# A fused linear-attention layer on one core: three reorderings and a last projection split in columns

## What is computed

```python
xn = layernorm(x)                                   # over the width
q, k, v = (silu(xn @ W) for W in (Wq, Wk, Wv))      # 16 heads of 16
# chunked linear attention with a decay per head, S carried over the chunks:
#   o = ((q k^T) * D) v  +  (q S) * q_decay ;  S = chunk_decay * S + (k * k_decay)^T v
o = o * sigmoid((xn @ Wg1) @ Wg2)                   # the gate
o = o * rsqrt(mean(o*o over the 16 of a head) + eps) * norm_w
s = o @ Wo
g = silu(fp8(xn * scale) @ fp8(W2 * scale1) / (scale * scale1))
out = x + s * g
```

## Time and profile before

| | |
|---|---|
| median of 3 runs | 128.74 us (128.6 to 129.91) |
| the profiled execution | 128.68 us, its span 126.9 us, so 1.78 us lie around the span |
| busy in the span | PE 114.7 us (90%), DVE 101.7 (80%), ACT 81.4 (64%), POOL 80.8 (64%) |
| granted TensorE clock | 0.99 of full speed over the span; the last fortieth of the span shows 7 tenths |
| DMA | 7.57 MB, mean 60 GB/s |
| steps 1 to 6 | VectorE makes og at 28.05, 41.56, 54.99, 68.40, 81.97, 95.32 and 108.68 us: 13.3 to 13.6 us a step |

### The profile page before, as it was taken

The page is one execution under the profiler, slowest core; times in us unless marked ns, Lnnn a source line. Parts: engine busy times, 40 slices in busy tenths (PEclk is TensorE's granted clock), DMA queues, the critical chain, the costliest instruction groups (busy, mean ns, idle before and its releaser), DMA issues.

```text
span 126.9 us, 6394 instructions
## 1 busy us (share of the span) xinstructions
PE 114.7 (90%) x2688; PEld 99.3 (78%) x2688; DVE 101.7 (80%) x271; ACT 81.4 (64%) x156; POOL 80.8 (64%) x119
## 2 busy tenths in 40 slices
PE   3979989988999999999999999999999999867680
PEld 3979889758978898879978898889788987556560
DVE  1899999989895899869994999498939891497781
ACT  7689989969967656684677378558673664811100
POOL 6716599899839683968677884968384839100070
PEclk9999999999999999999999999999999999999997
DMA  2769800020000400033003300150006040000015
GB/s 84 235 175 339 273 3 3 5 45 6 5 0 10 83 0 5 5 62 108 3 5 65 111 0 5 41 132 5 0 20 150 5 126 5 5 5 5 0 67 181
DMA packets 11067, 7.57 MB, mean 60 GB/s; under 512 B 4832, under 2 KB 11040, under 8 KB 11040
## 3 DMA queue, kind: packets, MB, share of 16 engines
q1 hardware_dynamic: 11040, 7.17, 20.2%
HBM read 3.50 MB, written 2.10 MB: 44 GB/s over the span
## 4 chain that ended last, share of the span: by engine, by line
POOL 31%; issue 29%; DVE 20%; ACT 9%; PE 6%; DMA 2%; POOLq 0%; DVEq 0%
POOL e_q L408 5%; POOL e_sum L403 5%; POOL y L441 5%; POOL kd L419 4%; DVE probs L764 4%; POOL rstd L396 3%; POOL own_mid L423 2%; POOL qd L413 2%; DMA x_sb<-in_L_attn_x_dram 2%; POOL on_lo L446 1%; PE b_s L1307 1%; DVE bn L729 1%; POOL own_end L423 1%; DVE og L797 1%; DVE xqT L754 1%
## 5 line engine op out<-in xcount | busy, mean ns | idle before, releaser
L1092 PE MATMUL b_kv<-w_hi,xT_hi 128*128 128x256 f32 x64 | 16.8, 284 | 0.0
L1093 PE MATMUL b_kv<-w_lo,xT_hi 128*128 128x256 f32 x64 | 16.5, 281 | 0.0
L441 POOL TENSOR_TENSOR y<-sg,x_sb 128x512 f32<-128x512 f32 x7 | 9.0, 1286 | 10.4 <-DVE sg L902 10.3
L446 POOL TENSOR_TENSOR on_lo<-on,on_hi 128x512 fp32r<-128x512 f32 x6 | 7.7, 1278 | 12.3 <-ACT on_hi L620 12.3
L403 POOL TENSOR_TENSOR e_sum<-e_y,e_magic 128x512 f32<-128x512 f32 x8 | 10.3, 1285 | 7.2 <-DVE e_magic L748 7.2
L797 DVE SCALAR_TENSOR_TENSOR og<-gate_tanh,b_o 128x512 f32<-128x512 f32 x7 | 4.8, 687 | 11.8 <-PE b_o L1243 11.8
L1095 PE MATMUL b_kv<-w_hi,xT_lo 128*128 128x256 f32 x64 | 12.7, 280 | 0.0
L1243 PE MATMUL b_o<-probs,v_par 64*32 64x64 f32 x896 | 12.6, 222 | 0.0
L413 POOL TENSOR_TENSOR qd<-q_silu,q_decay 128x512 f32<-128x512 f32 x8 | 10.3, 1293 | 3.3 <-ACT q_silu L550 3.3
L1092 PEld LDWEIGHTS b_kv<-w_hi,xT_hi 128*128 128x128 f32 x64 | 12.0, 188 | 0.2 <-issue 0.2
L1093 PEld LDWEIGHTS b_kv<-w_lo,xT_hi 128*128 128x128 f32 x64 | 12.1, 188 | 0.0
(11 more groups left out here) (205 smaller groups left out, 366.6 us busy)
## 6 DMA issues: line engine op xcount, KB each, us to landing
out_dram<-y SPq DMA_DIRECT2D x7, 256.0 KB, 2.5
x_sb<-in_L_attn_x_dram SPq DMA_DIRECT2D x4, 384.0 KB, 5.4
own_cross<-own_end SPq DMA_DIRECT2D x12, 64.0 KB, 2.0
qd_cross<-qd SPq DMA_DIRECT2D x12, 64.0 KB, 2.4
x_sb<-in_L_attn_x_dram SPq DMA_DIRECT2D x2, 256.0 KB, 3.5
w_f<-in_L_attn_Wq_dram SPq DMA_DIRECT2D x1, 256.0 KB, 3.8
w_f<-in_L_attn_Wk_dram SPq DMA_DIRECT2D x1, 256.0 KB, 4.0
w_f<-in_L_attn_Wv_dram SPq DMA_DIRECT2D x1, 256.0 KB, 4.5
```

The costliest lines, as they stand in the source:

```text
L441: g.tensor_tensor(y[:, n % 2], sg[:, n % 2].rearrange("p (s d) -> p s d", s=S), x_sb[:, x_tiles(n), :], ALU.add).then_inc(s_y, 1)
L446: g.tensor_tensor(on_lo[:], on[:, n % 2], on_hi[:].bitcast(F32), ALU.subtract).then_inc(s_onlo, 1)
L1092: t.matmul(dst[:, s], xT_hi[:, u, kk, tok], w_hi[:, w, kk], start=(s == 0 and kk == 0), stop=False, skip_group_check=True)
L1093: t.matmul(dst[:, s], xT_hi[:, u, kk, tok], w_lo[:, w, kk], start=False, stop=False, skip_group_check=True)
```

## The change

It has five parts. (1) In the steps 1 to 6 TensorE does the first quarter of the product with V (`from_chunk(n, 0, 0)`) ahead of `gate(n + 1)`, so that the gate's product stands next to `transpose_x(n + 2)`; step 6 has no transposes of x. (2) At the start ScalarE does `silu_v(0)` ahead of `silu_q(0)`, and `find_over(1)` ahead of `gate(1)`. (3) Still at the start, `gate_o(0)` goes ahead of `low_xT(2)` on VectorE, and `square_o(0)` ahead of `scale_y(2)` on ScalarE. (4) In step 7 VectorE does `gate_o(7)` ahead of `root_pair_last(6)`. (5) The last projection is done in three pieces (`LAST`): tile 0 whole, tile 1 in two halves of 128 columns, each with its own product, addition and store.

```diff
+        LAST = [(0, slice(0, D), b_s[:, 0:D], b_kv[:, 0:D]),
+                (1, slice(0, D // 2), b_s[:, 512:512 + D // 2], b_kv[:, 512:512 + D // 2]),
+                (1, slice(D // 2, D), b_o[:, 512:512 + D // 2], b_kv[:, 512 + D // 2:512 + D])]
...
-            for s in range(S):
-                sp.wait_ge(s_lasty, s + 1)
-                sp.dma_start(out_v[:, last.start + NB * s, :], y[:, 2, s]).then_inc(s_laststored, 16)
+            for m in range(len(LAST)):
+                s, cols, ps, prod = LAST[m]
+                sp.wait_ge(s_lasty, m + 1)
+                sp.dma_start(out_v[:, last.start + NB * s, cols], y[:, 2, s, cols]).then_inc(s_laststored, 16)
...
-            silu_q(0)
             act.wait_ge(s_vzero, 2)
             silu_v(0)
+            silu_q(0)
             high_xT(1)
...
+            find_over(1)
             gate(1)
-            find_over(1)
             high_xT(2)
             act.wait_ge(s_dvec, 4)
             silu_ffn(1)
+            square_o(0)
             scale_y(2)
-            square_o(0)
             silu_ffn(0)
...
             stats(3)
+            gate_o(0)
             low_xT(2)
-            gate_o(0)
...
             root_last(n - 1)
+            gate_o(n)
             root_pair_last(n - 1)
-            gate_o(n)
             head_norm(n - 1)
...
-            for s in range(S):
-                product_last(s)
-                add_x_last(s)
+            for m in range(len(LAST)):
+                product_last(m)
+                add_x_last(m)
...
+            def project_o_last(m):
+                n = STEPS - 1
+                s, cols, ps, prod = LAST[m]
+                pe.wait_ge(s_onlast, s + 1)
+                for kk in range(KH):
+                    mm = t.matmul(ps, on[:, n % 2, kk, s * P:s * P + P], wo_scaled[:, kk, cols], start=(kk == 0),
                                   stop=(kk == KH - 1), skip_group_check=True)
                 mm.then_inc(s_outps, 1)
...
                 state_steps(n)
+                from_chunk(n, 0, 0)
                 gate(n + 1)
-                from_chunk(n, 0, 0)
                 if known(n + 2):
                     transpose_x(n + 2)
```

More of the change, by code:

```diff
@@ L884, in head_norm_last, with product_last, add_x_last @@
                                 ps_rs.rearrange("p k (s c t) -> p s k c t", s=S, c=2)[:, s], ALU.mult).then_inc(s_onlast, 1)
-            def product_last(s):
+            def product_last(m):
                 n = STEPS - 1
-                dve.wait_ge(s_outps, n * S + s + 1)
+                s, cols, ps, prod = LAST[m]
+                dve.wait_ge(s_outps, n * S + m + 1)
                 dve.wait_ge(s_ffn, n + 1)
-                cols = slice(s * D, s * D + D)
-                v.tensor_tensor(ps_prod_last[s], ps_last[s], ffn_silu[:, n % 3, cols], ALU.mult).then_inc(s_lastsg, 1)
-            def add_x_last(s):
+                v.tensor_tensor(prod, ps, ffn_silu[:, n % 3, s * D + cols.start:s * D + cols.stop], ALU.mult).then_inc(s_lastsg, 1)
+            def add_x_last(m):
                 n = STEPS - 1
-                dve.wait_ge(s_lastsg, s + 1)
-                v.tensor_tensor(y[:, 2, s], ps_prod_last[s], x_sb[:, x_tiles(n).start + NB * s, :], ALU.add).then_inc(s_lasty, 1)
+                s, cols, ps, prod = LAST[m]
+                dve.wait_ge(s_lastsg, m + 1)
+                v.tensor_tensor(y[:, 2, s, cols], prod, x_sb[:, x_tiles(n).start + NB * s, cols], ALU.add).then_inc(s_lasty, 1)
             def product(n):
@@ L1279, in project_o @@
             def project_o(n, s):
-                if n == STEPS - 1:
-                    pe.wait_ge(s_onlast, s + 1)
-                elif s == 0:
+                if s == 0:
                     pe.wait_ge(s_on, n + 1)
@@ L1290, in project_o @@
                         pe.wait_ge(s_probs, 4 * STEPS)
-                dst = ps_out[:, s] if n < STEPS - 2 else ps_out_last2[:, s] if n < STEPS - 1 else ps_last[s]
+                dst = ps_out[:, s] if n < STEPS - 2 else ps_out_last2[:, s]
                 if n < STEPS - 2:
@@ L1306, in project_o @@
                 for kk in range(KH):
-                    mm = t.matmul(dst, on[:, n % 2, kk, s * P:s * P + P], wo_scaled[:, kk], start=(kk == 0 and (s == 0 or n == STEPS - 1)),
+                    mm = t.matmul(dst, on[:, n % 2, kk, s * P:s * P + P], wo_scaled[:, kk], start=(kk == 0 and s == 0),
+                                  stop=(kk == KH - 1), skip_group_check=True)
+                mm.then_inc(s_outps, 1)
+            def project_o_last(m):
+                n = STEPS - 1
+                s, cols, ps, prod = LAST[m]
+                pe.wait_ge(s_onlast, s + 1)
+                for kk in range(KH):
+                    mm = t.matmul(ps, on[:, n % 2, kk, s * P:s * P + P], wo_scaled[:, kk, cols], start=(kk == 0),
                                   stop=(kk == KH - 1), skip_group_check=True)
@@ L1413, in _ @@
             keep_warm(3, b_k)
-            for s in range(S):
-                project_o(n, s)
+            for m in range(len(LAST)):
+                project_o_last(m)
 _INS = ['L0_attn_x', 'L0_attn_log_decay', 'L0_attn_Wq', 'L0_attn_Wk', 'L0_attn_Wv', 'L0_attn_Wo', 'L0_attn_Wg1',
```

4 lines of the change are left out of this document (1 added, 3 removed).

## The result

| | before | after |
|---|---|---|
| median | 129.17 us (4 runs, 128.6 to 129.91) | 131.59 us (4 runs, 130.57 to 132.2) |
| ratio | | 1.0197, 95% interval 1.0128 to 1.0266 |
| the profiled execution | 128.68 us, span 126.9 | 132.2 us, span 130.5 |

The change costs 2.4 us. The forecast was 129.5 (+0.8), its range ended at 130.4: the sign was right, the size was not. The two profiled executions lie 3.5 apart, more than the medians: that of before is among the fastest of its kernel, that of after is the slowest of four. (A ratio leaves out executions more than 1.5% above the fastest of their kernel; where the clock falls in some executions of a kernel, that cuts some of these, so the medians over all stand beside the ratios.)

The account below looks back on a forecast made before the run. The prediction took a ring of og, VectorE and TensorE branches, then TensorE alone, to bound full steps. From 128.68 us, -0.4 (full steps) + 0.2 (start) + 0.9 (step 7) + 0.1 (tail) gave 129.5; range 128.5 to 130.4.

Parts of the forecast that it names:

- the 1.07: Step 7, TensorE: work in us from the load of spread_rs(6) to that of the head sums, without idle time.
- Rival C: Step 7: TensorE's clock falls after 1.8 us idle, work behind doubles, +2.2 us, 131.7 us; chance 0.05.
- The arrival of 0.3 of xT_hi's lateness: Start: xT_hi comes 0.4 us later, of which 0.3 reaches the projections of step 1.
- takes back: Start: find_over(1) ahead of the tanh recovers up to 0.48 us; xqT taken as 0.2 earlier than 25.98.
- the ring: Full steps: og, VectorE to last probs beside TensorE to state_steps, then TensorE alone to next og; at most 0.75 us saved.
- the only thing late next: Full steps: on_lo's slack of 0.12 us in step 2 limits the gain to 0.065 each in four steps.
- Rival A: Only full steps and start count as meant: 0.75 and 0.3 us saved, end costs 1.0, 128.6 us; chance 0.18.
- covered: Tail: part of the third store's 0.5 us later issue is hidden by the DMA queue ahead; +0.1 us taken.
- rival B: Tail: third store issue is on the path, +0.5 us; with start +0.5 too, 130.2 us; chance 0.16.

Follow-up runs that it names:

- e7_sums_first: Kernel before with og of step 7 ahead of root_pair_last(6), plus head_sums(7) on TensorE ahead of spread_rs(6) and project_o(5, 1); 130.37 us against 129.76, ratio 1.0073.
- e6_warm: Kernel before with part 4, plus six products on nothing on TensorE ahead of spread_rs(6) in step 7; 131.11 us against 129.76, ratio 1.0107.
- e2_start: Kernel before with parts 2 and 3 alone, the start of the program; 129.3 us against 129.06, ratio 1.0037.
- e3_full: Kernel before with part 1 alone, first quarter of the product with V ahead of the gate; 129.11 us against 129.06, ratio 1.0016.
- e5_silu: Kernel before with one line of part 2 alone, silu_v(0) ahead of silu_q(0); 129.85 us against 129.76, ratio 1.0034.
- e8_defer: Kernel before with part 1, plus the third quarter of the product with V ahead of transpose_k and the output projection; 129.41 us against 129.76, ratio 0.9981.
- e1_step7: Kernel before with part 4 alone, og of step 7 ahead of root_pair_last(6); 131.1 us against 129.06, ratio 1.012.
- e4_tail: Kernel before with part 5 alone, last projection in three pieces with three stores; 129.57 us against 129.06, ratio 1.0022.
- e10_more: Kernel before with 48 small products on nothing in place of the 10 at the very start; 129.78 us, ratio 1.0029.

## Why the prediction was wrong, point by point

**Part 4, the largest miss.** The failed step is "The head sums start at 116.74 + 1.07 = 117.81 instead of 116.91: +0.9 us", with bounds from +0.8 to +1.1. The mechanism was right: the order of TensorE held the head sums (e7_sums_first) and the 1.07 was nearly right (1.15 in e6_warm). Wrong was the 116.91 it was measured against. It is the value of an execution in which the product with V stood still for only 0.15 us. Of the five other profiles of the old order with the standstill at the 83rd product, four (e2_start, e3_full, e5_silu, e8_defer) have 0.6 us or more; there the old order hides the three root instructions and is 0.5 better. The term is +1.4, not +0.9: 3.05 us from the last product to the head sums instead of 1.66, and 1.4 us by the ratio in both sets with the gap filled.

**Rival C, given 0.05.** The second failed step: the sum put the clock at nothing. The granted clock did fall to the lower level behind the idle time that I had named (1.8 us forecast, 1.7 in the profile's brackets), in 16 of 22 executions with the new order. What it cost was not 2.2 but 0.4 to 1.1 us in the traces and up to 0.9 on the mean of the executions, since most of `project_o(6)` at the low level lies beside ScalarE's roots and VectorE's chain. That the earlier trace rows show no fall was no evidence: these rows had no such idle time.

**Parts 2 and 3.** I took +0.2, between -0.3 and +0.5, and the traces have 0.34 + 0.1 = +0.4 (e2_start, by the ratio, +0.5 with 0 to 0.9). The arrival of 0.3 of xT_hi's lateness was right. The failed step is the next one, that what `find_over(1)` "takes back" counts in the sum. For xqT itself it did take back the lateness: xqT starts 9.56 us behind the last probs of step 0 before, 9.87 in e5_silu (the swap alone), 9.48 in after and 9.50 in e2_start. But xqT comes at 25.95 and not at 25.78, and nothing behind it gained: from the gate of step 0 to the last probs of step 1 the time is no shorter than in e5_silu. It is 0.1 longer, where the late e_y puts the masks at 30.70 instead of 30.5.

**Part 1.** -0.4 was forecast, the traces have nothing. The failed step is "What is saved on TensorE behind this point is therefore saved in the ring, until something else is late there", with on_lo taken for the only thing late next. transpose_k of the next step also waits for state_end on VectorE, and did so already before the change. These rows of step 2 of the kernel before say it; I had not read them together:

```profile
50.73 0.61 DVE L788 SCALAR_TENSOR_TENSOR state_end<-state_mid,chunk_decay,b_kv 128x128 f32<-128x128 f32 x2
```

```profile
51.48 0.63 PE L1155 MATMUL b_kv<-ident,k_nat 128*128 128x128 f32 x4
```

51.48 is 0.146 behind 51.34, and that distance is the same, 0.145 to 0.147, in the steps 2, 3 and 5 of before, of e3_full and of e1_step7. TensorE was on time to a hair, so no idle time was put down to the wait. In step 1 on_lo held it (the load 0.05 behind the end of on_lo, as estimated). Step 4, where TensorE came 0.26 behind state_end before the change and so had room, gained 0.12 against the kernel before (5.32 us instead of 5.45 from the last probs to og). But the sum shows none of it: the steps 1 to 5 take 5.30 to 5.33 us in e3_full and 5.31 to 5.35 in e5_silu, whose old order was disturbed least (5.31 to 5.45 in before), and from og of step 0 to og of step 6 are 80.59 us in e3_full, 80.63 in before and 80.52 in e5_silu. e3_full's ratio of 1.0016 (0.9986 to 1.0047) agrees, and leaves out -0.4. Rival A, which needed the full 0.75, is refuted.

**Part 5.** +0.1 was forecast; the traces of e4_tail and of after have 5.77 us from the last projection to the end, of before 5.61: +0.2 (by the ratio +0.3, -0.2 to +0.7). The stores, answering to the earlier trace rows, in after:

```profile
127.38 1.44 SPq L381 DMA_DIRECT2D out_dram<-y  x3
...
out_dram<-y SPq DMA_DIRECT2D x2, 64.0 KB, 1.7
```

Counted from the start of the last projection, the last issue ends 0.5 later and the smaller transfer lands in 1.7 us instead of 2.0: the third issue is on the path and the bytes give 0.3 back. The failed step is a small one, that the 0.5 is "covered" by the queue ahead. The traces refute rival B, the whole 0.5; the time alone would not. The estimate from the Trainium skill, page DMA: Bandwidth & Descriptors, section Anatomy of one DMA (2.15 us to landing), is above the 1.7 measured.

**The sum.** +1.4 (part 4), +0.4 (start), 0 (full steps), +0.2 (tail) are +2.0, and the clock adds 0.4 to 1.1 in the executions in which it falls; the medians differ by 2.4. The order of step 7 and the clock behind it are thus the bulk of the miss. The profiled execution of after is longer by another 0.9 us in its full steps, which no part of the change is shown to cause; half of that is the one longer standstill of step 4. What the recorded range left out was a spread of the kernel before itself: I noted that the profiled execution lay 0.06 under the median of three and neglected it, where 35 further runs on one chip have a median of 129.06 and reach from 128.28 to 130.95, and 29 on another have one of 129.76.

## What to carry to other kernels

A slack read from one execution is the slack of that execution. Before an instruction is moved ahead of others "because its engine waits anyway", look whether what it overtakes is what fills a wait that is longer in other executions. An engine that comes exactly when its operand is released shows no idle time, so before a saving is booked, compare the start of each waiting instruction with the end of every one of its producers: a distance that is the same to a few ns in all steps, while the distance to the engine's own instruction before varies, is a wait. And idle time that is added to TensorE late in a kernel has a second price in its clock; products on nothing in that time kept the clock up in 11 executions of 12. Part 4 then cost 1.4 and 1.6 us by the medians instead of 2.0 and 2.7, on small sets.

## What the runs showed of the hardware

TensorE's instructions reach it in transfers of 16 KB on a queue of their own. The page of after has them in its list of queues, 21 of them with 0.34 MB; that each holds 256 instructions is worked out from the standstills, whose numbers lie multiples of 256 apart (within 2), and fits the 5511 instructions that the trace has of TensorE (e10_more, with 5655, has 22 transfers):

```profile
q8 instruction: 21, 0.34, 1.2%
```

Where small products run by the dozen, TensorE uses them up faster than they come: the 128 weight loads and 128 products with V of step 7 start within 1.5 us. The last four transfers of before start at 104.74, 108.30, 111.83 and 115.39 us, 3.5 to 3.6 apart, each taking about 0.9 to 1.1 and in other runs up to 1.5; TensorE went on from the 83rd product 1.2 to 1.5 us behind the end of the third. The standstill (over the 0.03 of an undisturbed distance) was 0.12 to 1.3 us in thirteen traces; in e10_more the next part of the program had it. Products on nothing at the very start of the program, more of them or fewer, move it. It differs from execution to execution of one kernel (distances of 0.70 and 1.32 us in the two profiles of part 4 alone), and I take it for a large part of the spread of the times; that was not measured by itself. Whether a shorter instruction stream in steps 6 and 7 would take it away was not tried.

A change of tile shape is not always a cost to be saved. From the last start of a quarter to a product of another shape are 0.15 us. Where two quarters follow each other (step 5 of e8_defer) the distance is only 0.03, but the starts of the second then spread over 0.38 us instead of 0.24, so that the two together take as long as with the change between them.
